# Edge loads of a graph convolution issued by two queues instead of one

## The chip, the cores and the metric

The kernel runs on one core of one Trainium2 chip. The metric is the device time of one execution in microseconds (us), as the median of several runs. Five engines work side by side, each with its own instruction queue: TensorE (PE), VectorE (DVE), ScalarE (ACT), GpSimd (POOL) and SyncE (SP). SP does no arithmetic. It waits on semaphores and issues DMA transfers. ACT and POOL can issue transfers as well, between their own instructions.

## The reference, cut to what matters

Four graph layers run one after another over 12,500 nodes and 200,000 edges, which are sorted by their target node. The change lies in the second one:

```python
z = concatenate([atom_features[dst], atom_features[src], edge_features], axis=1)   # 64 + 64 + 64
signal = softplus(batchnorm(z @ W_core.T + b_core))
gate = sigmoid(batchnorm(z @ W_filter.T + b_filter))
message = gate * signal
out = atom_features + segment_sum(message, dst)
```

`edge_features` has 64 floats for each of the 200,000 edges. The batch normalization needs the mean and the variance over all edges, so the layer is computed in two passes.

## The kernel before

The edges are cut into steps of 128, and eight steps make a group (`G = 8`). There are 208 groups, which are handled in 104 pairs. The **edge stage** is the first pass of the second layer: for each group it forms `z @ [W_core, W_filter]`, stores it to the DRAM tensor `y_stash`, and sums it and its square. All buffers come in rings, of two groups (`b = 0, 1`) or of four (`q = 0..3`). For a pair of groups the engines do this:

- **SP** (`l1_pair`, `load_edges`): for each of the two groups it waits until the edge features of the group four before are used up (`s.l1_transposed`, L568), reads eight start rows from a table into registers (`load8`, L424), and issues eight loads of 128 edges, 32 KB each, into `ea_s` (L562). Then it waits for the stores of the pair before and says so to DVE (`s.l1_stored`, L573). At last it waits for each of the two new groups (`s.l1_made`) and stores it (L577).
- **POOL** (`gathers`, L681): eight indirect gathers of 128 rows for each group, for a group four ahead. A group's gathers wait for its indices (`s.l1_indices`, from ACT's L801) and for the buffer (`s.l1_rows_used`, from DVE).
- **PE**: `l1_products` of a group (L1103, L1104), then `l1_transposes` of the group two ahead (L1089 for the one-hot matrices, L1091 for the edge features). This is done once for `b = 0` and once for `b = 1`. The transposes wait for the group's edge loads (`e_in[q]`) and for DVE's one-hot matrices.
- **ACT**: `l1_copies` of the two groups (L810, L811), which waits for the transposes. Then for each of the two groups `next_indices` (L801) and the square (L824), which waits for DVE.
- **DVE** (`l1_sums`): the one-hot matrices of two groups (L458), then for each group the sum that makes it (L1519, `s.l1_made`), the masked copy (L1525) and the running sum (L1529), and at last the sums of squares (L1534).

The wait in front of L1519 is this:

```python
dve.wait_ge(s.l1_stored, g + 1)
dve.wait_ge(s.l1_products, g + 1)
rows_landed(dve, i, q, 0)
```

So DVE can't make a pair before SP has issued the 16 loads that stand ahead of `s.l1_stored` in its queue. POOL's next 16 gathers wait for DVE's L1519 (`s.l1_rows_used` is raised right behind it) and for ACT's L801.

Of the kernel before, what the change touches and what calls it, by code (L numbers as in the profile page):

```python
# [14 lines left out]
P = 128  # L15
N = 12500
E = 200000
# [13 lines left out]
G = 8  # L31
# [3 lines left out]
ITER = S // PAIR  # L35
# [7 lines left out]
RING = 4  # L43
# [13 lines left out]
CHUNKS = W // WPC  # L57
WPP = 2 * WPC
PAIRS = W // WPP
NODE_AT = (0, PAIRS, PAIRS + CHUNKS, PAIRS + 2 * CHUNKS, 2 * PAIRS + 2 * CHUNKS)  # L60
# [15 lines left out]
def build(nc, x, src, dst, ea16, ea64, w_edge, b_edge, w_node, b_node,  # L76
          w_filter, b_filter, gamma_f, beta_f, w_core, b_core, gamma_c, beta_c,
          w_att, a_att, w1, b1, w2, b2, out):
    with ExitStack() as ctx:
# [3 lines left out]
        def sem(name):  # L83
            return ctx.enter_context(nc.semaphore(name))
# [25 lines left out]
        win_s, row_s, rel_s = (place_s[k * 32:k * 32 + 1, :] for k in range(3))  # L110
# [65 lines left out]
        ea_s = aux_flat[:, 3 * G * P:5 * G * P].rearrange("p (q u f) -> p q u f", q=4, u=G)  # L176
# [32 lines left out]
        def by_bank(ap):  # L209
# [112 lines left out]
            "edges_in1",  # L322
            "edges_in2",
            "edges_in3",
            "y_stored0",
            "y_stored1",

# [70 lines left out]
        s = namedtuple("Semaphores", NAMES)(*[sem(n) for n in NAMES])  # L398
        fill = [s.lane_done0, s.lane_done1, s.lane_done2, s.lane_done3]
        y_in = [s.l1b_y_in0, s.l1b_y_in1, s.l1b_y_in2, s.l1b_y_in3]  # L400
        index_in = [s.l2_index_in0, s.l2_index_in1, s.l2_index_in2, s.l2_index_in3]
        dst_in = [s.l2_dst_in0, s.l2_dst_in1, s.l2_dst_in2, s.l2_dst_in3]
        e_in = [s.edges_in0, s.edges_in1, s.edges_in2, s.edges_in3]
        rows_in = [s.rows_in0, s.rows_in1, s.rows_in2, s.rows_in3]

# [17 lines left out]
        def load8(engine, table, g, top):  # L423
            _, v = nc.values_load_multi_w_load_instructions(  # L424
                table[:, bass.ds(g * G, G)], engines=(engine,), min_val=0, max_val=top,
                skip_runtime_bounds_check_because="the table's entries are clamped to it")
            return v
# [3 lines left out]
        def load_steps(g, places=g_places, stride=P // 2, n=D, ring=LONG):  # L431
            _, v = nc.values_load_multi_w_load_instructions(
                places[:, bass.ds(g * GP, GP)], engines=(mybir.EngineType.PE,), min_val=0, max_val=(ring * G - 1) * n,
                skip_runtime_bounds_check_because=PLACES_WHY)
            tops = [(G - 1) * stride] * G + [(ring * G - 1) * n] * G
            v = [nc.s_assert_within(a, 0, t, skip_runtime_bounds_check_because=PLACES_WHY) for a, t in zip(v, tops)] + [
                nc.s_assert_within(v[2 * G], RING + 1, RING * (TT + 1))]
            return v[0:G], v[G:2 * G], v[2 * G]

        def load_rows(g):  # L440
            _, v = nc.values_load_multi_w_load_instructions(
                l2_places[:, bass.ds(g * GP + G, G + 1)], engines=(mybir.EngineType.Activation,), min_val=0, max_val=(L2_RING * G - 1) * D2,
                skip_runtime_bounds_check_because=PLACES_WHY)
            return v[0:G], nc.s_assert_within(v[G], RING + 1, RING * (TT + 1))

        def load1(engine, table, g, top):
            _, v = nc.values_load_multi_w_load_instructions(  # L447
                table[:, bass.ds(g * G, 1)], engines=(engine,), min_val=0, max_val=top,
                skip_runtime_bounds_check_because="the table's entries are clamped to it")
            return v[0]  # L450
# [30 lines left out]
        def _(sp):  # L481
# [75 lines left out]
            y_out = [s.y_stored0, s.y_stored1]  # L557

            def load_edges(g, q):
                starts = load8(mybir.EngineType.SP, row_s, g, E - P)  # L560
                for u in range(G):
                    sp.dma_start(ea_s[:, q, u, :], ea64[bass.ds(starts[u], P), :]).then_inc(e_in[q], 16)  # L562

            def l1_pair(i, half, first):
                for b in range(2):
                    g = i * 2 + b
                    sp.wait_ge(s.l1_transposed, g + 1)
                    sp.sem_inc(s.passed, 1)  # L568
                    load_edges(g + 4, 2 * half + b)
                if not first:  # L570
                    for b in range(2):
                        sp.wait_ge(y_out[b], i * 16)
                        sp.sem_inc(s.l1_stored, 1)  # L573
                for b in range(2):
                    g = i * 2 + b
                    sp.wait_ge(s.l1_made, g + 1)
                    sp.dma_start(y_stash[bass.ds(g, 1), :, :].rearrange("a p f -> (a p) f"),  # L577
                                 buf_c[:, b, :, :].rearrange("p u f -> p (u f)")).then_inc(y_out[b], 16)

            for q in range(4):  # L580
                load_edges(q, q)
# [6 lines left out]
                sp.wait_ge(y_out[b], ITER * 16)  # L588
            sp.sem_inc(s.l1_stored, 2)
            for q in range(4):  # L590
                sp.wait_ge(e_in[q], (ITER // 2 + 1) * G * 16)


            def load_y(g, q):
# [6 lines left out]
            with sp.Fori(0, ITER // 2 - 1) as i:  # L601
                for q in range(4):
                    g = i * 4 + q
# [116 lines left out]
        def _(act):  # L720
# [60 lines left out]
            with act.Fori(0, ITER - 1) as i:  # L781
                for b in range(2):
                    g = i * 2 + (b + 1)
# [11 lines left out]
            def indices(ready, table=src_s):  # L795
                for q in range(RING):
                    act.activation(idx[:, q, :], table[:, q * G:q * G + G], ACT.Copy).then_inc(ready, 1)

            def next_indices(i, q, ready, stage, table=src_s):
                rows_landed(act, i, q, stage)  # L800
                act.activation(idx[:, q, :], table[:, bass.ds(i * (RING * G) + (RING * G + q * G), G)], ACT.Copy).then_inc(ready, 1)  # L801
# [3 lines left out]
            node_copies(NODE_AT[1], x_n)  # L805
            indices(s.l1_indices)

            def l1_copies(g, b):
                act.wait_ge(s.l1_transposed, g + 1)
                act.activation(buf_d[:, b, :, :].rearrange("p u f -> p (u f)"), ps[:, b, :].bitcast(BF16), ACT.Copy)  # L810
                act.activation(buf_a[:, b, 0:4, :].rearrange("p u f -> p (u f)"), ps[:, 2 + b, :], ACT.Copy).then_inc(s.l1_trans_copied, 1)  # L811

            for b in range(2):
                l1_copies(b, b)
            with act.Fori(0, TURNS) as i:
                for half in range(2):
                    for b in range(2):
                        l1_copies(i * RING + (2 * half + b + 2), b)
                    for b in range(2):
                        q = 2 * half + b  # L820
                        next_indices(i, q, s.l1_indices, 0)
                        act.wait_ge(s.l1_masked, i * RING + (q + 1))
                        act.wait_ge(s.l1_sq_added, i * RING + (q + 1))
                        act.activation(sq[:, b, :, :], yv[:, b, :, :], ACT.Square).then_inc(s.l1_squared, 1)  # L824
# [35 lines left out]
            def l2_columns(g, q):  # L860
                at, needed = load_rows(g)
                act.wait_ge(s.l2_landed, needed)
                act.wait_ge(s.l2_scored, g + 1)
                for u in range(G):
                    last = act.activation(s_cols[:, q % 2, u:u + 1], l2_ring[:, bass.ds(at[u] + D1, 1)], ACT.Copy)
                last.then_inc(s.l2_columns, 1)
# [60 lines left out]
        def _(pe):  # L927
# [154 lines left out]

            def l1_transposes(turn, q, g):
                b = q % 2
                pe.wait_ge(e_in[q], turn * (G * 16) + G * 16)
                pe.wait_ge(s.l1_hot, g + 1)
                ob_ps = ps[:, b, :].bitcast(BF16)
                for u in range(G):
                    pe.transpose(ob_ps[:, u * P:u * P + P], ob[:, b, u, :], ident_b[:, :])  # L1089
                for u in range(G // 2):  # L1090
                    last = pe.transpose(ps[:, 2 + b, u * P:u * P + P],  # L1091
                                        ea_s[:, q, 2 * u:2 * u + 2, :].rearrange("p a f -> p (a f)"), ident[:, :])
                last.then_inc(s.l1_transposed, 1)

            for b in range(2):
                l1_transposes(0, b, b)
# [10 lines left out]
            with pe.Fori(0, ITER // 2) as i:  # L1107
                for half in range(2):
                    for b in range(2):
                        l1_products(i * 4 + (2 * half + b), b)  # L1110
                        l1_transposes(i + half, 2 * (1 - half) + b, i * 4 + (2 * half + b + 2))
# [710 lines left out]
```

## Time and profile before

| | |
|---|---|
| time, median of 3 runs | 15060.8 us (15028.1 to 15099.16) |
| time of the profiled execution | 15005.17 us |
| its span | 15003.3 us |
| edge stage in it | 3484 to 6483 us, 2999 us |
| busy in the stage from 3532 to 6483 us (2951 us) | POOL 1643 us, PE 1551 us, DVE 1321 us, ACT 553 us |
| granted TensorE clock in that stretch | 0.71 |
| share of the 16 DMA engines in that stretch | 0.32, 92 GB/s |

The span runs from the first to the last instruction of the profiled execution. No engine is busy for more than 56% of the edge stage, so the stage is a matter of who waits for whom. "SPq", "ACTq" and "DVEq" in the rows are the queues of these engines: instructions that only handle registers, semaphores or DMA issues. In a timeline a row is `start, duration, engine, line, operation, tiles, xcount`, and the brackets give the idle time in front of it and what ended it.

### The profile page before, as it was taken

To read this page: it belongs to the slowest core of one execution; us is meant where nothing else is said; L and a number is where in the kernel's file an instruction comes from. 1 tells how busy PE (TensorE), PEld (TensorE's weight loads), DVE (VectorE), ACT (ScalarE), POOL (GpSimd) and SP (SyncE) were. 2 spreads that over 40 slices of the span, in tenths; PEclk is the share of its full clock that TensorE was granted. 3 is DMA by queue.
4 is the path that set the end of the run, shared out by engine and by line. 5 is a ranking of instruction groups with operands and counts; after the bars stand their busy time and mean duration, and the time that the engine had idled before them with its cause. 6 is when DMAs were issued, how large, how long until landed. Compare 5 with 4: busy or idle time off the path is not lost.

```text
span 15003.3 us, 181666 instructions
## 1 busy us (share of the span) xinstructions
PE 8287.5 (55%) x46670; PEld 7635.5 (51%) x46671; DVE 6679.2 (45%) x13205; ACT 2744.9 (18%) x6542; POOL 9034.8 (60%) x8046
## 2 busy tenths in 40 slices
PE   5777777754555555578856555563333334333334
PEld 5777777754444444467745455463333333333333
DVE  6444444434444444479956556574222223222223
ACT  0111111101111111156633334341000000000000
POOL 3888888874555555510017777774666664666664
PEclk7666666667677777789967767675555555555555
DMA  5333333332333333333212222231111111111111
GB/s 91 18 18 18 18 18 18 18 50 80 91 91 92 91 91 91 91 100 99 98 49 69 64 66 71 63 79 31 23 23 23 23 23 26 23 23 23 23 23 23
DMA packets 851085, 769.36 MB, mean 51 GB/s; under 512 B 652784, under 2 KB 660804, under 8 KB 848965
## 3 DMA queue, kind: packets, MB, share of 16 engines
q0 software_dynamic: 446272, 333.87, 16.8%
q1 hardware_dynamic: 371597, 322.68, 6.8%
q10 hardware_dynamic: 33170, 112.27, 2.3%
q8 instruction: 21, 0.34, 0.0%
q14 instruction: 25, 0.20, 0.0%
HBM read 569.49 MB, written 197.82 MB: 51 GB/s over the span
## 4 chain that ended last, share of the span: by engine, by line
issue 23%; another core or an unknown queue 18%; PE 13%; DVE 12%; SPq 10%; POOL 10%; DMA 9%; DVEq 4%; ACT 0%; ACTq 0%; POOLq 0%
POOL lane_tab L667 8%; DMA lane_tab<-rows,idx 8%; SPq L562 7%; PE ps L1129 3%; PE ps L1144 3%; DVE buf_c L1519 2%; SPq L424 2%; DVE acc_w L1773 1%; DVEq L447 1%; DVEq L458 1%; PE ps L1232 1%; PE ps L1213 1%; PE ps L1168 1%; PE ps L1154 1%
## 5 line engine op out<-in xcount | busy, mean ns | idle before, releaser
L691 POOL DMA_INDIRECT tab<-gcn_tab,idx x3136 | 2986.0, 952 | 1718.5 <-issue 1148.2
L667 POOL DMA_INDIRECT lane_tab<-rows,idx x1664 | 2599.8, 1562 | 616.2 <-issue 613.5
L691 POOL DMA_INDIRECT tab<-att_tab,idx x1568 | 1762.5, 1124 | 1928.3 <-DVEq L1660 1330.1
L1144 PE MATMUL ps<-tab,buf_d 128*128 x3328 | 794.4, 387 | 2171.3 <-issue 2118.7
L1144 PEld LDWEIGHTS ps<-tab,buf_d 128*128 128x128 f32 x3328 | 782.0, 320 | 2283.8 <-issue 2283.7
L1773 DVE TENSOR_TENSOR acc_w<-acc_w,ps 128x512 f32 x416 | 286.3, 688 | 3422.0 <-remote 2957.1
L681 POOL DMA_INDIRECT buf_b<-src_tab,idx x832 | 834.2, 1003 | 802.5 <-DVEq L1522 339.5
L681 POOL DMA_INDIRECT acc_w<-src_tab,idx x832 | 840.0, 1010 | 654.9 <-DVEq L1522 399.9
L1103 PE MATMUL ps<-tab,buf_d 128*128 x3328 | 892.6, 361 | 354.5 <-DVEq L1523 331.7
L1043 PE MATMUL ps<-ident,srcg 128*128 128x128 f32 x3328 | 723.1, 405 | 656.2 <-DVE srcg L1406 653.5
L1144 PEld LDWEIGHTS ps<-tab,buf_a 128*128 128x128 f32 x3328 | 726.0, 330 | 652.9 <-issue 652.6
L1144 PE MATMUL ps<-tab,buf_a 128*128 x3328 | 762.8, 424 | 534.1 <-issue 446.3
L1043 PEld LDWEIGHTS ps<-ident,srcg 128*128 128x128 f32 x3328 | 669.3, 307 | 705.5 <-DVE srcg L1406 701.4
L1103 PEld LDWEIGHTS ps<-tab,buf_d 128*128 128x128 f32 x3328 | 738.7, 274 | 393.0 <-issue 392.5
L1104 PE MATMUL ps<-wte,buf_a 128*128 128x128 f32 x3328 | 858.2, 348 | 137.4 <-issue 136.8
L801 ACT ACTIVATE idx<-gate_s 128x8 int32 x392 | 81.8, 209 | 4427.2 <-DMA tab<-gcn_tab,idx 4427.2
L1060 PE MATMUL ps<-tab,buf_d 128*128 x3328 | 878.2, 355 | 0.0
L1213 PE MATMUL ps<-ident,tmp_c 128*128 128x128 f32 x3328 | 560.5, 333 | 392.7 <-issue 286.7
L1104 PEld LDWEIGHTS ps<-wte,buf_a 128*128 128x128 f32 x3328 | 722.1, 266 | 104.1 <-issue 104.0
L1232 PE MATMUL ps<-tab,buf_d 128*128 x3328 | 516.4, 319 | 435.0 <-issue 401.0
L1089 PE MATMUL ps<-ident_b,aux 128*128 128x128 bf16 x1680 | 234.0, 288 | 942.5 <-issue 790.2
L1213 PEld LDWEIGHTS ps<-ident,tmp_c 128*128 128x128 f32 x3328 | 536.0, 249 | 424.4 <-issue 411.9
(283 smaller groups left out, 17226.4 us busy)
## 6 DMA issues: line engine op xcount, KB each, us to landing
y_stash<-buf_c SPq DMA_DIRECT2D x208, 512.0 KB
tab<-y_stash SPq DMA_DIRECT2D x208, 512.0 KB, 3.3
aux<-in_edge_attr_dram SPq DMA_DIRECT2D x1696, 32.0 KB
aux<-dst_rows ACTq DMA_DIRECT2D x104, 512.0 KB
buf_b<-dst_rows ACTq DMA_DIRECT2D x104, 512.0 KB
tab<-gcn_tab,idx POOLq DMA_INDIRECT x3136
lane_tab<-rows,idx POOLq DMA_INDIRECT x1664
tab<-att_tab,idx POOLq DMA_INDIRECT x1568
```

The source lines that it names most:

```text
L562: sp.dma_start(ea_s[:, q, u, :], ea64[bass.ds(starts[u], P), :]).then_inc(e_in[q], 16)
L667: pool.indirect_dma_start(lane_tab[k][:, :], bass.IndirectOffsetOnAxis(ap=idx[:, b, u:u + 1], axis=0), rows[:, b, u, 0:D1], None, compute_ ...
L681: pool.indirect_dma_start(to[q][:, u, :], None, table[:, :], bass.IndirectOffsetOnAxis(ap=idx[:, q, u:u + 1], axis=0)).then_inc(rows_in[q] ...
L691: pool.indirect_dma_start(to[k][:, u, :], None, table[:, :], bass.IndirectOffsetOnAxis(ap=idx[:, k % RING, u:u + 1], axis=0)).then_inc(row ...
L1043: last = pe.matmul(region(8 * b + u, P), bc(srcg[:, b, u:u + 1], [P, P]), ident[:, :], start=True, stop=True)
L1060: last = pe.matmul(region(o, D), buf_d[:, b, u, :], window(tab, ws[u], D), start=True, stop=True)
L1103: pe.matmul(o, buf_d[:, b, u, :], window(tab, ws[u], P), start=True, stop=False)
L1104: last = pe.matmul(o, buf_a[:, b, u // 2, :], wte[:, u % 2, :], start=False, stop=True)
L1129: last = pe.matmul(ps_flat[:, bass.ds(rel[u] + bank * 512, n)], left[:, u, :], right[:, u, 0:n], start=False, stop=True, skip_group_check= ...
L1144: last = pe.matmul(ps_flat[:, bass.ds(rel[u] + q * 512, D)], g_hot[q][:, u, :], g_ring[:, bass.ds(at[u], D)], start=False, stop=True, skip ...
L1213: last = pe.matmul(region(u, P), bc(s_cols[:, q % 2, u:u + 1], [P, P]), ident[:, :], start=True, stop=True)
L1232: last = pe.matmul(ps_flat[:, bass.ds(rel[u] + bank * 512, D1)], l2_hot[q % 2][:, u, :], l2_ring[:, bass.ds(at[u], D1)], start=False, stop ...
```

## The change

The first four of a group's eight edge loads stay with SP. The last four are issued by ACT, ahead of the two `l1_copies` of each pair. ACT reads its own four start rows for them. Each ring slot gets a second semaphore (`more_in`), and PE waits for both.

```diff
+        def load_starts(engine, g, first):
+            _, v = nc.values_load_multi_w_load_instructions(
+                row_s[:, bass.ds(g * G + first, G // 2)], engines=(engine,), min_val=0, max_val=E - P,
...
             def load_edges(g, q):
-                starts = load8(mybir.EngineType.SP, row_s, g, E - P)
-                for u in range(G):
+                starts = load_starts(mybir.EngineType.SP, g, 0)
+                for u in range(G // 2):
                     sp.dma_start(ea_s[:, q, u, :], ea64[bass.ds(starts[u], P), :]).then_inc(e_in[q], 16)
...
+            def load_more_edges(g, q):
+                starts = load_starts(mybir.EngineType.Activation, g, G // 2)
+                for u in range(G // 2):
+                    act.dma_start(ea_s[:, q, G // 2 + u, :], ea64[bass.ds(starts[u], P), :]).then_inc(more_in[q], 16)
...
+            act.wait_ge(s.node_products, NODE_AT[1] + CHUNKS + 2)
+            for q in range(4):
+                load_more_edges(q, q)
             for b in range(2):
                 l1_copies(b, b)
             with act.Fori(0, TURNS) as i:
                 for half in range(2):
+                    for b in range(2):
+                        load_more_edges(i * RING + (2 * half + b + 4), 2 * half + b)
                     for b in range(2):
                         l1_copies(i * RING + (2 * half + b + 2), b)
...
             def l1_transposes(turn, q, g):
                 b = q % 2
-                pe.wait_ge(e_in[q], turn * (G * 16) + G * 16)
+                pe.wait_ge(e_in[q], turn * (G * 8) + G * 8)
+                pe.sem_inc(s.passed, 1)
+                pe.wait_ge(more_in[q], turn * (G * 8) + G * 8)
                 pe.wait_ge(s.l1_hot, g + 1)
```

SP's waits at the end of the stage are halved in the same way and get the second semaphore too.

## Rows read from the trace of the kernel before

**Rows 1.** Waits, 3600 to 6400 us: who waited for whom, us, times, longest.
```profile
DVE buf_c L1519 <- SPq L573: 1454.2, 97, 15.9
...
POOL buf_b L681 <- DVEq L1522: 331.2, 41, 8.9
...
POOL buf_b L681 <- ACT idx L801: 49.5, 8, 6.4
```

**Rows 2.** Line L1519, every second pair: ns min/median/max, first and last start.
```profile
L1519 DVE TENSOR_TENSOR buf_c<-ps,acc_w x104: 1216/1221/1226, 3567.6 to 6481.5; 128x1024 f32<-128x1024 f32 x104
```

**Rows 3.** Timeline of DVE, first L1519 of two successive pairs.
```profile
5000.26 1.23 DVE L1519 TENSOR_TENSOR buf_c<-ps,acc_w 128x1024 f32<-128x1024 f32 x1 [14.63 <-SPq L573]
...
5029.33 1.22 DVE L1519 TENSOR_TENSOR buf_c<-ps,buf_b 128x1024 f32<-128x1024 f32 x1 [15.38 <-SPq L573]
```

**Rows 4.** Timeline of SP in the same pair.
```profile
5001.65 4.32 SPq L577 DMA_DIRECT2D y_stash<-buf_c  x2
5008.09 20.89 SPq L562 DMA_DIRECT2D aux<-in_edge_attr_dram  x16
```

**Rows 5.** Chain of waits, 5006 to 5030 us: start, us, what.
```profile
5010.57 0.70 SPq L562
...
5017.70 0.69 SPq L562
...
5019.10 0.69 SPq L567
...
5024.00 0.70 SPq L562
...
5025.52 0.33 SPq L562
...
5026.04 0.33 SPq L562
```

**Rows 6.** Timeline of POOL: first, sixth and last gather, and the next pair's first.
```profile
5002.35 1.53 POOL L681 DMA_INDIRECT acc_w<-src_tab,idx  x1 [7.54 <-DVEq L1522]
...
5009.41 0.95 POOL L681 DMA_INDIRECT acc_w<-src_tab,idx  x1 [0.30 <-issue]
...
5021.98 0.95 POOL L681 DMA_INDIRECT acc_w<-src_tab,idx  x1 [0.30 <-issue]
5031.43 1.53 POOL L681 DMA_INDIRECT buf_b<-src_tab,idx  x1 [8.50 <-DVEq L1522]
```

**Rows 7.** Timeline of ACT in the same pair.
```profile
5000.13 0.21 ACT L801 ACTIVATE idx<-src_s 128x8 int32 x1
...
5007.06 1.06 ACT L824 ACTIVATE aux<-acc_w 128x1024 f32<-128x1024 f32 x1 [2.81 <-DVE acc_w L1525]
5019.85 1.02 ACT L810 ACTIVATE buf_d<-ps 128x1024 f32<-128x1024 bf16 x1 [11.73 <-remote]
...
5027.24 1.02 ACT L810 ACTIVATE buf_d<-ps 128x1024 f32<-128x1024 bf16 x1 [5.88 <-PE ps L1091]
...
5028.64 0.21 ACT L801 ACTIVATE idx<-src_s 128x8 int32 x1
```

**Rows 8.** Timeline of PE: the last transposes of the pair.
```profile
5026.14 1.06 PE L1091 MATMUL ps<-ident,aux 128*128 128x128 f32 x4
```

**Rows 9.** Timeline, 5774 to 5780 us: an L801 and the gather behind it.
```profile
5775.95 0.21 ACT L801 ACTIVATE idx<-src_s 128x8 int32 x1
...
5777.07 1.53 POOL L681 DMA_INDIRECT buf_b<-src_tab,idx  x1 [6.21 <-DVEq L1522]
```

**Rows 10.** Line L562, 3600 to 6400 us: SP's other instructions for a load.
```profile
L562 SPq FUSED_REGOPS  x1561: 2/37/1402, 3604.2 to 6399.7; - x196
L562 SPq MOVE aux<-in_edge_attr_dram x1560: 2/29/1390, 3604.3 to 6392.6; - x195
```

**Rows 11.** Line L865 of a later stage, 8533 to 8546 us: ACT's register instructions.
```profile
L865 ACTq FUSED_REGOPS  x8: 16/48/702, 8540.9 to 8545.2; - x8
```

**Rows 12.** Timeline of SP at the start of the stage.
```profile
3484.39 51.78 SPq L562 DMA_DIRECT2D aux<-in_edge_attr_dram  x34
```

More of the change, by code:

```diff
@@ L324, in build @@
             "edges_in3",
+            "more_in0",
+            "more_in1",
+            "more_in2",
+            "more_in3",
             "y_stored0",
@@ L402, in build @@
         dst_in = [s.l2_dst_in0, s.l2_dst_in1, s.l2_dst_in2, s.l2_dst_in3]
+        more_in = [s.more_in0, s.more_in1, s.more_in2, s.more_in3]
         e_in = [s.edges_in0, s.edges_in1, s.edges_in2, s.edges_in3]
@@ L444, in load_rows @@
             return v[0:G], nc.s_assert_within(v[G], RING + 1, RING * (TT + 1))
+        def load_starts(engine, g, first):
+            _, v = nc.values_load_multi_w_load_instructions(
+                row_s[:, bass.ds(g * G + first, G // 2)], engines=(engine,), min_val=0, max_val=E - P,
+                skip_runtime_bounds_check_because="the table's entries are clamped to it")
+            return v
         def load1(engine, table, g, top):
@@ L590, in _ @@
             for q in range(4):
-                sp.wait_ge(e_in[q], (ITER // 2 + 1) * G * 16)
+                sp.wait_ge(e_in[q], (ITER // 2 + 1) * G * 8)
+                sp.wait_ge(more_in[q], (ITER // 2 + 1) * G * 8)
             def load_y(g, q):
```

## Prediction

> **What bounds the kernel now.** I first read the busy table and the stretches (no engine fills the edge stage), then the list of waits in it. Its largest row is DVE's L1519 waiting for SP's L573, 97 times, 1454.2 us [rows 1]: SP says late that the old stores are done, because 16 edge loads stand ahead of that in its queue. One pair repeats every (6481.5 - 3567.6 - 4)/102 = 28.5 us, where 4 us is the distance of a pair's two L1519 [rows 2]. The timelines of one pair show the order. The first L1519 runs at 5000.26 and the next pair's at 5029.33, after 15.38 us of idling [rows 3]. SP issues its loads from 5008.09 to 5028.98 [rows 4].
>
> The loads take 20.89 us because SP's queue has two speeds. From 5025.52 on, one load follows another after 0.52 us. Between about 5010.1 and 5025.4, each single instruction of SP, register moves too, takes a turn of 0.70 us [rows 5]. That slow stretch begins with the sixth gather of POOL's row of 16 (5009.41) and ends some 2.5 us behind the last one (5021.98 + 0.95) [rows 6]. I call it the slow stretch; why gathers slow the other queues, no row shows. A load is three instructions of SP (a register operation, a move, the DMA) [rows 4, 10], so it costs 0.52 us outside the stretch and 2.1 us inside. The stretch has 15.3/0.70 = 22 turns. SP's pieces account for 17, and the rest go mostly to PE, so I take the turns to be shared between the queues that want them.
>
> POOL's next gathers start 2.10 us behind L1519 (5031.43 - 5029.33) [rows 3, 6]. So the loop is now: L1519, gathers, slow stretch, rest of SP's loads, L573, L1519.
>
> **What the change removes.** SP loses 8 loads of 3 instructions per pair. Of its remaining work, about 4 loads still run before the slow stretch. Then come two waiting or register instructions, the second table read and 4 loads, 16 instructions, which need 16 of the 22 turns. Before, SP had 7 loads left when the stretch ended (3.6 us). Now it has between none (if it gets the turns) and three (if it gets a third of them, 7: 9 instructions left). L573 comes 2.1 to 3.6 us earlier. If nothing else bound, the stage would gain 101 x 2.1 to 3.6 = 210 to 360 us. The end is not there, because the next wait is close.
>
> **What is late next.** POOL's gathers need ACT's L801 too. It runs at 5028.64, after the copies of both groups, and the second copy (5027.24) can't start before PE's last transposes end at 5026.14 + 1.06 = 5027.20 [rows 7, 8]. Those transposes sit in the slow stretch and finish 1.8 us behind its end; the change doesn't touch them. Where L801 is the last (at 5775.95), the gather follows after 1.12 us (5777.07) [rows 9]. So in the pair shown the gathers could start at 5028.64 + 1.12 = 5029.76 at the earliest, 1.67 us before they do; in the pair before it, 5002.35 - 5000.13 - 1.12 = 1.10 us before [rows 6, 7]. The mean is 1.39 us. In 8 of about 98 pairs L801 is already named as what the gathers waited for [rows 1], and there is nothing to win: 1.39 x 90/98 = 1.27 us per pair. That is the ceiling as long as ACT's copies are not late.
>
> **What the change adds.** ACT gets 2 table reads and 8 loads, about 28 instructions. They stand behind the last square (5007.06) and ahead of the copy that now starts at 5019.85, and in between ACT has idled for 11.73 us [rows 7]. At the free rate they take 8 x 0.52 + 2 x 1.0 = 6.2 us, all hidden in that gap. But from 5010.1 on they fall into the slow stretch, and ACT's queue isn't spared by such stretches: in a later stage its register instructions take up to 702 ns [rows 11]. ACT's price for an edge load is not shown. I bound it by SP's two prices, 0.52 and 2.1 us. By 5010.1 ACT has issued some 10 of the 28; 17 remain, beside SP's 16 and PE's 5, for 22 turns. Some 16 instructions are left over, 7 of them ACT's: two loads and a bit, 1.2 us. The copies have 0.2 us to spare (first copy 1.6 us, transposes 1.8 us behind the end of the stretch), so they would be 1.0 us late. Against that works that the pair now starts earlier against its gathers: L1519 would lie some 3 us ahead of the first gather instead of 2.1. SP and ACT then each get one to two loads more out before the stretch begins, 26 to 30 instructions stay for 22 turns, and ACT has at most one load left. I take a delay of 0.4 us; the ends are 0 (ACT is through in time) and 2.5 us (it gets no turn for its second table read and its last four loads: 4 x 0.52 + 0.6, less 0.2).
>
> The two more instructions of PE per group fall where PE waits anyway. The semaphore, the transfers themselves (the DMA engines are busy for 0.32 of the stretch) and the order of landing, two pairs ahead of use, cost nothing.
>
> At the start of the stage SP takes 51.78 us for 34 loads, most of it slow [rows 12]. ACT's first 16 loads now stand ahead of its first copies there. That costs once, 0 to 10 us, and I take 5.
>
> The Trainium skill, page "DMA: Bandwidth & Descriptors", section "Issuing engines are not separate DMA queues", says that issuing from several engines only saves the sequencer's issue time, which is usually small relative to the DMA itself. By that rule alone the change would be worth nothing. The trace agrees with the mechanism and not with the size here, since the issue time of 20.89 us is what DVE waits for [rows 4].
>
> **Sum.** 1.27 - 0.4 = 0.87 us per pair, times 101 pairs with gathers behind them, is 88 us; less 5 is 83 us. Against the profiled execution, 15005 - 83 = 14922 us. The median of the runs lies 56 us above the profiled one, so I carry the difference over: 15060.8 - 83 = 14978 us.
>
> **The rivals.**
> *No gain, since the turns are shared.* If the turns of the slow stretch are what is scarce, moving instructions to another queue wins little: ACT ends 1.0 to 1.5 us late and takes back what SP gave. The gain is 1.27 - 1.0 = 0.27 us or less per pair, -27 to +25 us in all, about 15050. For it speaks that PE's and SP's pieces alternate in the stretch; against it, the earlier start.
> *One generator for both queues.* If the DMA instructions of SP and ACT exclude each other (0.33 us each, [rows 5]), the free part before the stretch holds fewer loads: 8 loads take 2.7 us instead of 2.1. That is 0.6 us less per pair, 83 - 61 = 22 us of gain, about 15040. No row has both issuing at once. The Trainium skill, page "Perfetto Trace Analysis", section on the HWDGE DMA instruction, describes one descriptor block that a sequencer locks for exclusive use; by it this rival would hold.
> *Slower: the copies wait for ACT's loads.* The second table read and the last four loads of ACT stay behind the slow stretch. Then both copies, L801 and the gathers start 2.5 us late: 1.27 - 2.5 = -1.23 us per pair, 124 us slower, about 15185. It decides from a delay of 1.27 us on, that is from three of ACT's loads left over. For it speaks the count 17 + 16 + 5 against 22 turns, against it that ACT has idled long enough before to have instructions in hand.
>
> **How the numbers follow.** 0.5%, about what a measurement of this kernel can tell from no change, is 75 us. The forecast (delay 0 to 0.6 us, 63 to 123 us faster) gets 0.5, shared turns 0.25, the generator 0.08, slower 0.17. A part of the forecast's lower end, 0.03, lies within 75 us. So faster 0.47, same 0.36, slower 0.17. The range goes from the forecast's best, 14938 less 40 us for the scatter of the runs, to half way into the slower case: 14895 to 15115.
>
> **What would show it.** After the change, DVE's wait for SP's L573 should be much shorter or gone, and POOL's waits should name ACT's L801 far more often. SP's 8 loads should end by about 2 us behind the slow stretch. A pair should take some 27.6 us. The first L810 of a pair shows the delay: at or before the second transposes' end the forecast holds, 1.3 us or more behind it the slower rival. The forecast would be wrong if the slow stretch grows with the traffic of two hardware queues, or if L573 stays the last wait.

## The result and the profile after

| | before | after |
|---|---|---|
| median, 4 runs each | 15079.98 us (15028.1 to 15122.59) | 14889.45 us (14847.87 to 14940.95) |
| profiled execution | 15005.17 us | 14940.95 us |
| edge stage in it, first edge load of SP to last sum | 3484.4 to 6481.5, 2997 us | 3533.7 to 6345.6, 2812 us |

The ratio is 0.9879, 95% interval 0.985 to 0.9908: the changed kernel is about 1.2% faster. That is 191 us by the medians, and the forecast was 83 us. The measured median lies 5.6 us below the lower end of the range.

In the profiled execution the edge stage is 185 us shorter. The stage starts 49 us later there than before, and the stages after it take 72 us more. Other executions below also start it at either 3485 to 3489 or 3525 to 3536 us, whichever kernel they run, so the start is not the change's doing. The 72 us appear in this one pair of profiles only, and I leave them open. The profiled execution is also the slowest of the four after.

The list of waits of the changed kernel, 3600 to 6400 us (who waited for whom, us, times, longest), answers to [rows 1]:

```profile
ACT buf_d L827 <- remote: 1766.6, 124, 27.1
DVE buf_c L1543 <- remote: 787.3, 88, 19.4
...
POOL acc_w L693 <- ACT idx L813: 335.1, 51, 13.4
ACT buf_d L827 <- PE ps L1115: 332.8, 71, 24.5
...
POOL buf_b L693 <- ACT idx L813: 282.0, 45, 9.3
DVE buf_c L1543 <- issue: 262.4, 37, 22.4
...
DVE buf_c L1543 <- PE ps L1128: 244.4, 38, 12.6
```

L1519 is now L1543, and no row names its wait for SP any more. POOL's gathers wait for ACT's index conversion (L801, now L813) 96 times and 617 us, against 8 times and 49.5 us. That is the wait that the prediction named as the next.

But DVE idles in front of its sums nearly as long as before, 787.3 + 262.4 + 244.4 = 1294.1 us against 1454.2; it only idles elsewhere. Before, all of it stood in front of the first sum of a pair. Now the first sums have 396 us of it, 41 of 102 without a wait, and the second sums, which had none, have 895 us. "remote" and "issue" name no cause, so I put the recorded ends of the three things that a sum waits for (SP's step, PE's products, the rows) beside its start. 37 second sums start behind PE's products (L1128). For the 65 others, 663 us, all three were there before, and 50 of these start 2.0 to 3.1 us behind the end of a row of gathers, where the slow stretch ends. An example:

```profile
4839.83 1.22 DVE L1553 TENSOR_TENSOR acc_w<-acc_w 128x1024 f32<-128x1024 f32 x1
4854.19 1.22 DVE L1543 TENSOR_TENSOR buf_c<-ps,acc_w 128x1024 f32<-128x1024 f32 x1 [13.14 <-remote]
```

The group's products end at 4842.65 and POOL's row at 4850.94 + 0.95 = 4851.89; the sum starts 2.30 us behind that. So in the changed kernel DVE too stands still in slow stretches, although nothing that the trace records holds it; whether its own queue is slow there or a semaphore reaches it late, the trace doesn't tell. The prediction has no such term, and no run separates it. Nor is SP's word always in time. The 19.39 us of idling in the long pair below end 0.3 us behind SP's step (4904.28 and 4904.32). And 42 first sums start up to 3.35 us before the trace records the step that they wait for, so the recorded times of SP's instructions in a slow stretch can lag by that much, and whether SP was the last there stays open.

The lines of the sum, every second pair (answers to [rows 2]):

```profile
L1543 DVE TENSOR_TENSOR buf_c<-ps,buf_b x104: 1207/1224/1226, 3581.7 to 6326.8; 128x1024 f32<-128x1024 f32 x104
L1543 DVE TENSOR_TENSOR buf_c<-ps,acc_w x104: 1210/1225/1226, 3596.9 to 6345.6; 128x1024 f32<-128x1024 f32 x104
```

With 4.9 us between the last pair's two sums, a pair takes (6345.6 - 3596.9 - 4.9)/102 = 26.9 us, where it took 28.5. But the mean hides the new picture. Before, the pairs (counted from the sixth on, without the last) took 27.5 to 29.5 us. Now they take 13.7 to 41.0 us, in an uneven pattern: 16 of them are over 34 us, and 5 of these 40.8 us or more. Two successive pairs in the timelines show one of the five and the short pair behind it. DVE's sums open pairs at 4863.78, 4904.62 and 4920.19, so these pairs take 40.84 and 15.57 us.

```profile
4863.78 1.21 DVE L1543 TENSOR_TENSOR buf_c<-ps,buf_b 128x1024 f32<-128x1024 f32 x1
...
4904.62 1.22 DVE L1543 TENSOR_TENSOR buf_c<-ps,acc_w 128x1024 f32<-128x1024 f32 x1 [19.39 <-remote]
...
4920.19 1.21 DVE L1543 TENSOR_TENSOR buf_c<-ps,buf_b 128x1024 f32<-128x1024 f32 x1
```

POOL's gathers in the same stretch: the second of a row of 32, its last, and the next row's first (between the first two lines shown lie 29 more, with 0.3 us between one and the next):

```profile
4859.59 1.94 POOL L693 DMA_INDIRECT acc_w<-src_tab,idx  x1 [1.78 <-issue]
...
4899.59 0.95 POOL L693 DMA_INDIRECT buf_b<-src_tab,idx  x1 [0.30 <-issue]
4913.95 1.53 POOL L693 DMA_INDIRECT acc_w<-src_tab,idx  x1 [13.41 <-ACT idx L813]
```

SP's loads, then ACT's:

```profile
4857.70 4.74 SPq L573 DMA_DIRECT2D aux<-in_edge_attr_dram  x8
...
4875.49 28.76 SPq L573 DMA_DIRECT2D aux<-in_edge_attr_dram  x8
...
4914.12 5.86 SPq L573 DMA_DIRECT2D aux<-in_edge_attr_dram  x8
```

```profile
4879.75 24.84 ACTq L823 DMA_DIRECT2D aux<-in_edge_attr_dram  x7
4905.01 1.03 ACT L827 ACTIVATE buf_d<-ps 128x1024 f32<-128x1024 bf16 x1 [24.46 <-PE ps L1115]
...
4914.40 4.36 ACTq L823 DMA_DIRECT2D aux<-in_edge_attr_dram  x8
```

And PE's transposes:

```profile
4889.58 0.26 PE L1113 MATMUL ps<-ident_b,aux 128*128 128x128 bf16 x1 [2.54 <-issue]
4892.38 0.27 PE L1113 MATMUL ps<-ident_b,aux 128*128 128x128 bf16 x1 [2.53 <-issue]
...
4904.30 0.67 PE L1115 MATMUL ps<-ident,aux 128*128 128x128 f32 x2 [1.04 <-issue]
```

SP's eight loads take 4.74 or 5.86 us where they miss the slow stretch, and 28.76 us where they fall into a long one. Rows of gathers with a pause of over 2 us between them are counted in the trace: before, 102 rows of 16 and one of 32, at the start of the stage; after, 92 of 16 and 6 of 32. Five of these six fall into the five pairs of 40.8 to 41.0 us.

In the slow stretch PE is slow too. A transpose is a weight load and a matmul, two instructions 1.40 us apart, so the matmuls come 2.80 us apart. SP's and ACT's instructions also mostly come 1.40 us apart there (4891.65, 4893.05, 4894.45), and the two start within 0.01 us of one another. ACT's copy (L827, the old L810) at 4905.01 starts 0.04 us behind PE's last transposes, and ACT's own loads are through at 4904.59. So the copy waits for PE. That ACT's loads are what slowed PE is not shown: in the kernel before, where ACT issues none, PE's instructions are 1.40 us apart as well, from 5019.83 to 5025.42, beside SP's.

I counted the slow turns in the trace: two successive starts in one queue, other than POOL's, 0.67 to 0.73 or 1.37 to 1.43 us apart; PE's queue holds its weight loads and its matmuls. From first sum to last, before: SP 1565, PE 620, ACT 3, together 2188. After: SP 966, PE 975, ACT 110, DVE 31, together 2082. SP lost 599 of them, and the other queues took 493 back.

That queues slow one another shows in the same count. In the changed kernel 143 of PE's 644 slow turns without one of another queue beside them are of the 1.40 us kind, and 178 of 283 beside SP's. But turns aren't a simple share of one resource. In the kernel before, PE starts 99 instructions from 5012.42 to 5019.12, at most 0.21 us apart, while SP starts nine in the same 6.7 us.

### The profile page after: what moved, and what is told of

It is laid out like the page before. It is cut to its first block, busy times and chain, and to the rows that moved or that the text cites. A ratio compares the mean times of both kernels' runs of the same rounds, so it can differ in the third digit from the quotient of the medians.

```text
span 14939.1 us, 182194 instructions
## 1 busy us (share of the span) xinstructions
PE 8307.1 (56%) x46670; PEld 7582.8 (51%) x46671; DVE 6695.0 (45%) x13205; ACT 2723.1 (18%) x6542; POOL 8996.6 (60%) x8046
## 4 chain that ended last, share of the span: by engine, by line
issue 23%; another core or an unknown queue 19%; PE 18%; POOL 15%; DVE 10%; DMA 8%; DVEq 5%; ACT 1%; ACTq 0%; POOLq 0%; SPq 0%
POOL lane_tab L679 9%; DMA lane_tab<-rows,idx 7%; POOL tab L703 6%; PE ps L1127 3%; PE ps L1153 3%; PE ps L1128 3%; DVEq L469 2%; DVE acc_w L1797 2%; DVEq L458 1%; DVE buf_d L469 1%; PE ps L1192 1%; PE ps L1178 1%; PE ps L1168 1%; PE ps L1113 1%
## 5 line engine op out<-in xcount | busy, mean ns | idle before, releaser
L1168 PEld LDWEIGHTS ps<-tab,buf_d 128*128 128x128 f32 x3328 | 781.0, 320 | 2249.3 <-issue 2249.3
L1128 PE MATMUL ps<-wte,buf_a 128*128 128x128 f32 x3328 | 854.7, 338 | 346.9 <-issue 344.6
L813 ACT ACTIVATE idx<-gate_s 128x8 int32 x392 | 81.7, 208 | 4427.3 <-DMA tab<-gcn_tab,idx 4427.3
L1127 PEld LDWEIGHTS ps<-tab,buf_d 128*128 128x128 f32 x3328 | 697.3, 253 | 373.9 <-issue 372.9
L1128 PEld LDWEIGHTS ps<-wte,buf_a 128*128 128x128 f32 x3328 | 691.2, 251 | 375.4 <-issue 375.0
L1256 PEld LDWEIGHTS ps<-tab,buf_d 128*128 128x128 f32 x3328 | 484.8, 231 | 532.3 <-issue 530.9
```

Source lines behind the costliest of these rows:

```text
L1127: pe.matmul(o, buf_d[:, b, u, :], window(tab, ws[u], P), start=True, stop=False)
L1128: last = pe.matmul(o, buf_a[:, b, u // 2, :], wte[:, u % 2, :], start=False, stop=True)
L1168: last = pe.matmul(ps_flat[:, bass.ds(rel[u] + q * 512, D)], g_hot[q][:, u, :], g_ring[:, bass.ds(at[u], D)], start=False, stop=True, skip ...
L1256: last = pe.matmul(ps_flat[:, bass.ds(rel[u] + bank * 512, D1)], l2_hot[q % 2][:, u, :], l2_ring[:, bass.ds(at[u], D1)], start=False, stop ...
```

## Experiments

The runs below were made on four different chips; which one the first comparison ran on is not recorded. On three of the four the kernel before takes only 13298, 13318 and 13314 us. So the first thing to settle was what these quicker chips lack. The numbers of turns and the pair times "counted" or "computed from the trace" below are made in the same way as above.

**The kernel before again, to have its profile on the quicker chips.** No edit.

> The kernel before, unchanged, to have its profile on the chip of the other runs. Theory A (the slow turns of 0.70 us belong to the chip of the first comparison or to its condition, and POOL's row of gathers only triggers them there): where the median is near 13,300 us, hardly a piece of SP's queue in the edge stage lasts 0.70 us, the 16 loads take under 12 us, a pair takes 20.6 us, and DVE's wait in front of L1519 is short; where the median is near 15,060 us, the picture is the known one with 28.5 us per pair. Theory B (the slow turns are everywhere, and the other chip is quicker for another reason): pieces of 0.70 us are as many at either median. The ratio is 1.00 within 0.3% either way.

Measured: 13338.59 us, ratio 1.0007 (0.9987 to 1.0026) to the other runs of the same kernel. Its sum, and SP and POOL in one pair:

```profile
L1519 DVE TENSOR_TENSOR buf_c<-ps,acc_w x104: 1216/1224/1226, 3528.1 to 5659.6; 128x1024 f32<-128x1024 f32 x104
...
  SPq L573: 320.1, 95
```

```profile
5007.17 8.21 SPq L577 DMA_DIRECT2D y_stash<-buf_c  x2
5017.38 8.93 SPq L562 DMA_DIRECT2D aux<-in_edge_attr_dram  x16
```

```profile
5025.32 0.95 POOL L681 DMA_INDIRECT acc_w<-src_tab,idx  x1 [0.30 <-issue]
5026.57 0.95 POOL L681 DMA_INDIRECT acc_w<-src_tab,idx  x1 [0.30 <-issue]
5027.82 0.94 POOL L681 DMA_INDIRECT acc_w<-src_tab,idx  x1 [0.30 <-DVEq L1522]
5029.06 1.02 POOL L681 DMA_INDIRECT acc_w<-src_tab,idx  x1 [0.30 <-issue]
```

The 16 loads take 8.93 us here against 20.89 [rows 4]. 61 slow turns are counted in the stage against 2188, a pair takes 20.9 us, and POOL never stops: its gathers follow one another by 0.3 us across the pairs. A gather costs the same on both chips (0.95 us). Theory A holds. DVE still waits for SP, 3.4 us each time, but nobody waits for DVE.

**The changed kernel again, on the same chip.** No edit.

> The changed kernel, unchanged, beside the kernel before on the same chip. Theory A (the gain is a gain of issue time in slow turns): on a chip without them POOL's gathers fill the pair (16 x 1.29 = 20.6 us), SP's loads are done long before they are wanted, and the ratio is 1.00 within 0.3%; on a chip with them the ratio is 0.985 to 0.991 again. Theory B (two queues load the edges faster whatever the turns): 0.985 to 0.991 on either.

Measured: 13338.49 us, ratio 1.0003 (0.9984 to 1.0021). DVE's waits, and SP's and ACT's loads of one pair:

```profile
  DMA buf_b<-src_tab,idx: 368.3, 104
  DMA acc_w<-src_tab,idx: 361.2, 104
```

```profile
5010.45 4.60 SPq L573 DMA_DIRECT2D aux<-in_edge_attr_dram  x8
...
5011.52 4.48 ACTq L823 DMA_DIRECT2D aux<-in_edge_attr_dram  x8
```

DVE waits for gathers only, the wait for SP is gone (95 times before), and the time is the same. The wait for SP was there, and removing it was worth nothing while POOL filled the pair. The two rows of loads also settle the rival of one generator: both queues issue at once from 5011.52 on (two of their DMA instructions start there within 0.01 us of one another and last 0.37 and 0.33 us, as long as one alone), and their eight loads take 4.60 and 4.48 us, about half of the 8.93 us that sixteen took in one queue.

**Four variants, on another quick chip (before: 13298.09 us).** Their expectations were worked out from pairs of 28.5 us, which that chip doesn't have.

```diff
 # stored first: in the kernel before
             def l1_pair(i, half, first):
+                if not first:
+                    for b in range(2):
+                        sp.wait_ge(y_out[b], i * 16)
+                        sp.sem_inc(s.l1_stored, 1)
...
                     load_edges(g + 4, 2 * half + b)
-                if not first:
-                    for b in range(2):
-                        sp.wait_ge(y_out[b], i * 16)
-                        sp.sem_inc(s.l1_stored, 1)
 # loads behind copies: in the changed kernel; "behind indices" puts them behind next_indices
-                    for b in range(2):
-                        load_more_edges(i * RING + (2 * half + b + 4), 2 * half + b)
                     for b in range(2):
                         l1_copies(i * RING + (2 * half + b + 2), b)
+                    for b in range(2):
+                        load_more_edges(i * RING + (2 * half + b + 4), 2 * half + b)
 # both halves on SP: in the changed kernel, in load_edges; ACT issues none
+                more = load_starts(mybir.EngineType.SP, g, G // 2)
+                for u in range(G // 2):
+                    sp.dma_start(ea_s[:, q, G // 2 + u, :], ea64[bass.ds(more[u], P), :]).then_inc(more_in[q], 16)
```

> The kernel before, all 16 loads of a pair on SP, but SP waits for the old stores and raises l1_stored ahead of them. Theory A (the change gains because DVE no longer waits for SP's word behind 16 loads): this gains too, though less than all of the wait, since the new store now stands behind the loads: 21 us of loads, 1 us of stores and 4 us until they land make some 27 us per pair instead of 28.65, 150 us faster than before. Theory B (the change gains because two queues get more of the slow turns): SP issues as slowly as before, so no more than 30 us either way.

Measured: 13280.98 us, 0.9981 (0.9961 to 1.0).

> The changed kernel with ACT's 8 loads between the two copies and the index copies. If POOL's gathers are now bound by ACT's index copies, they come some 6 us later per pair (28 instructions at the free rate): 300 to 600 us slower than the changed kernel. If something else bounds them, within 50 us of it.

Measured: 13319.93 us, 0.9991 (0.9972 to 1.001).

> The changed kernel with ACT's loads of a pair moved behind both copies and both index copies, each group's four ahead of its square. Theory A with ACT's indices as the new bound: copies and indices are never late now, but the squares are, by up to 6 us at the free rate, and DVE waits for them; the gathers start earlier. 0 to 100 us faster than the changed kernel. If the place of ACT's loads does not matter (theory B), within 40 us of the changed kernel (14890 us).

Measured: 13379.87 us, 1.0041 (1.0022 to 1.006).

> Control: everything of the change but the queue. Two table reads, two semaphores and PE's second wait, with all 16 loads on SP. Both theories: no gain. Four more SP instructions per pair, most of them at 0.7 to 1.4 us in the slow stretch, ahead of l1_stored: 1 to 4 us per pair, 100 to 400 us slower than before. A gain here would mean that the semaphores or the smaller table reads made the difference.

Measured: 13370.49 us, 1.0046 (1.0019 to 1.0073).

The first two have pairs of 20.6 us (computed from the trace). They move nothing, as POOL is the bound. The third is slower, and its list of waits, 3600 to 5600 us, says where:

```profile
ACT aux L847 <- issue: 278.1, 121, 2.4
...
DVE acc_w L1559 <- ACT aux L847: 144.9, 95, 1.7
```

ACT's squares stand behind its loads, and DVE's sum of squares (L1559) waits for them 1.5 us in every pair, with pairs of 21.3 us. So the place of the loads in ACT's order does matter; ahead of the copies, as in the change, they delay nothing there. The fourth costs 0.2 to 0.7%, 72 us by the medians. Its pairs take 20.9 us, 0.3 more than those of the first two on the same chip, which is about 30 us of it; the rest and the cause stay open. What it does show is that a second table read and a second semaphore are no source of a gain.

**Stored first and split together,** on the chip of the kernel before again.

> The changed kernel with SP's two l1_stored steps raised ahead of its loads, so that DVE never waits for a load to be issued. Theory A: on a chip with slow turns this gives what the split gives and a little more, ratio 0.975 to 0.99 (the loads are then late only for PE, two pairs on); on one without them 1.00 within 0.3%. Rival (what was gained came from the shorter queue of SP alone, and the wait for l1_stored was all of it): the same ratio as the changed kernel within 0.2%.

Measured: 13323.66 us, 1.0005 (0.9988 to 1.0021). As expected for such a chip; it can't tell there whether the shorter queue or the place of the step is what gains.

**One gather of eight.** In the kernel before; seven of eight gathers of the stage are left out, and the waits for the rows are scaled to it (not shown).

```diff
-                        for u in range(G):
+                        for u in range(1):
                             pool.indirect_dma_start(to[q][:, u, :], None, table[:, :],
```

> The kernel before with 1 of the 8 gathers of each group in the edge stage; the other seven are left out, and the waits for the rows are scaled to it, so the output is not the reference's. Theory A (a row of more than five gathers sets off the slow turns): no piece of 0.70 us is left in SP's queue on either kind of chip, the 16 loads take 8 to 12 us, and a pair is bound by PE, ACT and DVE: 15 to 18 us, 104 x (28.5 - 17) = about 1,200 us less than 15,060 (ratio 0.92) or 104 x (20.6 - 17) = about 375 us less than 13,300 (ratio 0.97). Rival (the slow turns come from the DMA traffic of the stores and loads, or from SP's and PE's queues together, and gathers only coincide with them): on a chip that has them SP's pieces of 0.70 us stay, and a pair is no shorter than 25 us.

Measured: 12930.02 us, 0.9697 (0.9663 to 0.9731), pairs of 16.9 us. It shows that POOL was the bound there and what lies beneath it. As to the trigger of the slow turns it is inconclusive: the chip had hardly any with the gathers either (28 counted against 61).

**Late loads, made on purpose.** As the quicker chips don't make SP late, the next three do it by hand, on the third quick chip (before: 13314.37 us). SP waits until every second load has landed:

```diff
                     sp.dma_start(ea_s[:, q, u, :], ea64[bass.ds(starts[u], P), :]).then_inc(e_in[q], 16)
+                    if u % 2:
+                        sp.wait_ge(e_in[q], turn * 128 + 16 * (u + 1))
+                        sp.sem_inc(s.passed, 1)
```

> The kernel before, in which SP waits after every second edge load until it has landed. That makes its 16 loads late on purpose, as the slow turns did in the first comparison. Theory A (what costs is only that l1_stored stands behind late loads): the loads take 20 to 28 us, and the pair takes that plus the 7.8 us from L1519 to the first load, 28 to 36 us, where it was 20.9; DVE's wait for SP in front of L1519 is the longest of its waits again, 10 us or more a pair; 14,050 to 14,900 us, ratio 1.055 to 1.12. Rival (the first chip was slow because of what the engines do, not because SP's loads were late): POOL still fills the pair, ratio under 1.02.

Measured: 14194.2 us, 1.0641 (1.0609 to 1.0673). SP's loads, and DVE's sum with what it waited for:

```profile
5005.81 19.13 SPq L562 DMA_DIRECT2D aux<-in_edge_attr_dram  x16
```

```profile
L1522 DVE TENSOR_TENSOR buf_c<-ps,buf_b x104: 1214/1223/1226, 3514.6 to 6509.9; 128x1024 f32<-128x1024 f32 x104
...
  SPq L576: 1596.2, 103
```

With 19.13 us of loads in place of 8.93, a pair takes 29.0 us in place of 20.9 (8.93 and 20.9 are from the quick chip above; the kernel before has no profile on this one). SP's wait is 15.5 us a pair, as in the first comparison [rows 3], and the whole picture of [rows 1 to 4] is there, with only 81 slow turns. So the place of late loads ahead of `l1_stored` is enough to make such a stage. The gathers come in the same 102 rows of 16 with pauses between them as in the first comparison, so on this chip such rows make no slow turns.

The same waits in the changed kernel, in SP's half alone:

> The changed kernel with the same waits in SP's half alone; ACT's loads are issued freely. Theory A: SP's 8 loads take 10 to 14 us, plus 7.8 is under POOL's 20.8 us, so POOL is the bound again, and nearly all that p1 lost is back: ratio 1.00 to 1.015. Rival (the split wins little, since the load time as such and not its place ahead of l1_stored counts): ratio within 1% of p1's.

Measured: 13372.82 us, 1.0015 (0.9995 to 1.0036). All but 0.15 of the 6.4% is back. SP's eight loads take 9.7 us, and POOL is the bound again.

And in both halves:

```diff
                     act.dma_start(ea_s[:, q, G // 2 + u, :], ea64[bass.ds(starts[u], P), :]).then_inc(more_in[q], 16)
+                    if u % 2:
+                        act.wait_ge(more_in[q], turn * 64 + 16 * (u + 1))
+                        act.sem_inc(s.passed, 1)
```

> The changed kernel with the waits in both queues: ACT's 8 loads take 10 to 14 us too, between its last square and its copies, where it idles for only 6.2 us on this kind of chip. Theory A with the limit that the prediction named (ACT's copies are the next bound): the copies come 4 to 8 us late, ACT's own round (loads, two copies 5.2 us apart, two squares 7 us apart) takes 23 to 28 us a pair, so the ratio lies between p2's and p1's, at 1.015 to 1.055, and ACT L827 starts right behind its loads, not behind PE's transposes. Rival (ACT's queue hides its loads): the ratio of p2.

Measured: 13313.52 us, 0.9999 (0.998 to 1.0019). My theory missed here. ACT in one pair:

```profile
5014.39 8.93 ACTq L826 DMA_DIRECT2D aux<-in_edge_attr_dram  x8
5025.22 1.03 ACT L833 ACTIVATE buf_d<-ps 128x1024 f32<-128x1024 bf16 x1 [10.64 <-DMA aux<-in_edge_attr_dram]
...
5026.61 1.03 ACT L833 ACTIVATE buf_d<-ps 128x1024 f32<-128x1024 bf16 x1
...
5027.99 0.23 ACT L816 ACTIVATE idx<-src_s 128x8 int32 x1
```

The first copy does wait for ACT's loads, as I expected. But the second follows 1.39 us behind it instead of some 5, because PE has its transposes of both groups ready by then. L816 comes 3.2 us behind the pair's first sum, and in the kernel before it was 3.8 us. I had added ACT's delay to a round that had slack between its two copies.

**Late loads, stored first.** The first of these three, with the `l1_stored` steps ahead of the loads (the diff of "stored first").

> The kernel with late loads all on SP, with one more edit: the two l1_stored steps stand ahead of the loads instead of behind them. No second queue. Theory A (it is the place of l1_stored behind the loads that costs): DVE no longer waits for the loads. SP's own round is then some 3 us for the stores of the pair before, 19.1 us of loads and 1 to 2 us for the two stores, 23 to 25 us a pair, between POOL's 20.8 and the 29 of the kernel with late loads: ratio 1.015 to 1.035 against the kernel before. If SP's round is no bound, 1.00 to 1.01. Rival (the loads themselves are late for PE, whichever way SP orders them): ratio 1.06 again, and PE's waits name the edge loads.

Measured: 15833.66 us, 1.0385 (1.0356 to 1.0414). This run was made on the fourth chip, which is of the slow kind: the kernel before takes 15248.61 us there. SP's queue and its chain of waits:

```profile
5024.74 0.92 SPq L580 DMA_DIRECT2D y_stash<-buf_c  x2
5029.76 28.71 SPq L562 DMA_DIRECT2D aux<-in_edge_attr_dram  x16
```

```profile
5017.58 0.70 SPq L562
5018.30 0.69 SPq L562
5018.98 0.70 SPq L565
5019.72 0.33 SPq L562
...
5025.31 3.40 DMA y_stash<-buf_c
```

The slow turns are back (1632 counted), here too until 2.4 us behind the last gather of a row (it ends at 5016.33 + 0.94 = 5017.27, and the last slow piece at 5019.68). With them the 16 loads take 28.71 us instead of 19.13, and SP's own round is the bound: 28.7 of loads, 1.7 until the stores, 0.9 for them and 4.1 until the next load, 35.4 us; the trace gives 35.1 a pair. DVE then waits for the raised `l1_stored` (2196 us in the stage), since SP is late as a whole. So with the order changed the queue's own length is the next bound. The numbers of the expectation were for a quick chip. What late loads alone, without the raised step, cost on a slow one wasn't run, so this run doesn't price the order. Nor was the raised step without late loads run on a slow chip: whether order alone, with no second queue, would have won what the change won in the first comparison is untested.

## Why the prediction was right, and where its sizes were off

**The bound before: right.** DVE waited for the loads ahead of `l1_stored`; from 3600 to 6400 us all 97 first sums start within 0.13 us behind SP's step. With late loads made by hand the picture came back (6.4% slower), and splitting those loads took it away (0.15%).

**SP's late loads come from slow turns that go with rows of gathers: right as read, its cause open.** They are there in the first comparison and on one chip of the experiments (2188 and 1632 counted in the stage), and nearly absent on the three others (at most 81). Without them the change is worth 1.0003. What makes them wasn't settled, and a kernel with fewer gathers on a slow chip wasn't run. The prediction's 22 turns, of which SP has 17 and PE most of the rest, were misread: PE started 99 instructions within 6.7 us of the same stretch.

**The next bound is ACT's L801: right for POOL.** 8 waits became 96.

**The ceiling of 1.27 us per pair: the term that was mis-sized.** The prediction took the slow stretch as a fixed part of every pair and 0.87 us as the gain. Measured are 28.5 - 26.9 = 1.6 us a pair, 163 us over 102 pairs. The distance from L801 to the gathers was read right, but in a loop in which the pair always met the stretch at the same place. With SP's queue shorter that lock is gone: some pairs run between two slow stretches in 14 to 17 us, others have to get through one of up to 41. That the lost lock is what makes the mean 1.6 and not 1.27 is read from the pairs' times, not shown by a run of its own.

**DVE's standing still in slow stretches: no term of the prediction.** It takes 663 us in front of 65 second sums, which by the trace had nothing left to wait for. The wait that the profile gives to SP is gone from the list, but DVE's idle time only fell from 1454 to 1294 us.

**ACT's delay of 0.4 us: its mechanism is not borne out.** The loads don't hold the copy directly in the pair shown; it waits 24.46 us, until PE's transposes are done, and these come 2.80 us apart. The rival of shared turns has a part in this: SP lost 599 turns, and the other queues have 493 more. But it is no end of the gain, as that rival had it. 106 turns fewer remain, and since the queues take them side by side, no time follows from that number. Whether the transposes would be quicker without ACT's loads wasn't run.

**The opening, 5 us of loss: wrong sign.** From the first load of SP to the second pair's first sum it took 3567.6 - 3484.4 = 83.2 us [rows 2, 12] and now takes 3596.9 - 3533.7 = 63.2, a gain of 20 us. SP's part in it:

```profile
3533.73 48.40 SPq L573 DMA_DIRECT2D aux<-in_edge_attr_dram  x24
```

24 loads in 48.40 us, no faster than 34 in 51.78 [rows 12]. But behind its first sums SP has only 8 loads left ahead of the second pair's step, and they took 4.44 us (from 3589.52 on); before it had 16, in 19.29 us (from 3548.24 on). 163 + 20 makes the 183 of the 185 us by which the stage shortened.

**One generator for both queues: fell on the quick chip.** Both issue at once, each at the pace that it has alone. In slow stretches it wasn't separated from the turns.

**Slower, as the copies wait for ACT's loads: fell.** Even loads that ACT itself waits for cost nothing, as far as POOL is the bound. On the slow kind of chip it wasn't tried alone.

**The range** is 3 us too low at its fast end by its own sum (14938 - 40 = 14898); the measured 14889.45 lies below either.

**The rule that issuing from another engine saves only issue time, which is usually small** (the Trainium skill, page "DMA: Bandwidth & Descriptors", section "Issuing engines are not separate DMA queues"): on the quick chip the trace agrees, ratio 1.0003. On the slow one issue time was 20.89 us of a pair of 28.5, and the split gained 1.2%.

## What to carry to other kernels

A queue's issue time costs what stands behind it in the same queue. Look for a cheap semaphore step behind a long row of DMA issues, and ask who waits for it, and then whether anybody waits for that one: on the quick chip DVE waited for SP in 95 pairs and it cost nothing. A ceiling that is read from one phase of a regular loop holds only while the loop keeps its phase. And the same kernel can have another bound on another chip, so read the profile of the chip on which the ratio was taken.

## What was not expected of the hardware

The same kernel took 15080 us in the first comparison and 15249 us on one chip, and 13298, 13318 and 13314 us on three others, 12% less. In the edge stage the difference is 2997 against 2175 us, and behind it 8522 against 7658. It doesn't lie in the work of the engines: the gathers (0.95 us) and the sums (1.22 us) last the same in both. In the edge stage it lies in the instructions of the queues other than POOL's, which on the slow kind take turns of 0.70 or 1.40 us beside rows of gathers, in several queues at once. Behind the stage PE's queue has 2007 such turns against 71; that they make up the difference there is argued, not shown.

What sets a chip into this condition, no run here shows. One rival is open beside the chip itself: the recording. All traces hold about the same number of instructions (180,210 to 183,248), but those of the slow kind hold 68,447 to 79,467 updates of semaphores, and the others 165,367 to 188,945. So a slow chip leaves less than half as many of these records, and SP's steps in the changed kernel are recorded up to 3.35 us late. The times of the runs before (15028 to 15123 us) are on the level of the profiled execution (15005 us); whether they were recorded in the same way is not known. Whether the slow turns lose the records, or writing the records makes the slow turns, wasn't tested.
